# Wide attention in a decoder kernel: a VectorE mask, exponentials with sums on ScalarE, and weights turned in a score bank

## What is computed

```python
    q = split_heads(x @ Wq)
    k = split_heads(x @ Wk)
    v = split_heads(x @ Wv)
    q = apply_rope(q)
    k = apply_rope(k)
    sim = jnp.einsum('bid,bjd->bij', q, k) * scale
    causal = jnp.tril(jnp.ones((t, t), dtype=bool))
    sim = jnp.where(causal[None], sim, -jnp.inf)
    attn = jax.nn.softmax(sim, axis=-1)
    out = jnp.einsum('bij,bjd->bid', attn, v)
    out = out.reshape(b, h, t, d).transpose(0, 2, 1, 3).reshape(b, t, h * d)
    return out @ Wo + bo
```

## Time and profile before

| | us |
|---|---|
| median of 3 runs | 1153.3 (1153.07 to 1155.71) |
| the profiled execution, its own time | 1154.45 |
| its span, first to last instruction | 1152.7 |
| the wide attention in it, about | 594 to 1012 |
| one block of four items in its loop | 24.03 and 24.14, in turn |

### The profile page before, as it was taken

How to read it: one execution, slowest core, us unless ns; L and a number is a source line. 1 busy time by engine, 2 the same in 40 slices (tenths; PEclk the granted TensorE clock), 3 DMA queues, 4 the chain that set the end, 5 groups by cost and what they waited for, 6 DMA issues and landing times. The chain is left out here.

```text
span 1152.7 us, 38659 instructions
## 1 busy us (share of the span) xinstructions
PE 995.0 (86%) x14758; PEld 803.4 (70%) x14759; DVE 844.9 (73%) x2021; ACT 588.4 (51%) x982; POOL 574.4 (50%) x711
## 2 busy tenths in 40 slices
PE   5999999999945799999947989999999999868464
PEld 2666666667632799999945878888888888746213
DVE  4878787888749244444426989999999999568686
ACT  3665656677720466666612444444444444447555
POOL 4232424353300433333225888888888886533424
PEclk9999999999965799999977999999999999955555
DMA  8200000000000111111230000000000000041002
GB/s 256 100 2 0 2 11 20 20 20 28 11 28 0 36 50 47 47 47 47 43 112 10 15 10 12 11 9 11 11 11 11 9 11 1 2 111 56 0 1 74
DMA packets 36985, 37.61 MB, mean 33 GB/s; under 512 B 7142, under 2 KB 31145, under 8 KB 36522
## 3 DMA queue, kind: packets, MB, share of 16 engines
q1 hardware_dynamic: 31690, 27.33, 7.8%
q0 software_dynamic: 4352, 8.92, 3.1%
q10 hardware_dynamic: 866, 0.33, 0.1%
HBM read 27.65 MB, written 8.91 MB: 32 GB/s over the span
## 5 line engine op out<-in xcount | busy, mean ns | idle before, releaser
L1283 POOL DMA_INDIRECT e_x<-xn_rows,e_where x72 | 68.1, 946 | 168.7 <-DVE e_where L1264 120.5
L360 POOL TENSOR_SCALAR n_KX<-n_KT,n_of_head 128x512 f32<-128x512 f32 x124 | 83.8, 698 | 122.0 <-ACT n_KT L601 85.2
L1253 DVE COPY e_y<-e_Y_ps 128x128 f32<-128x128 f32 x72 | 21.0, 291 | 113.8 <-PE e_Y_ps L1220 112.5
L760 DVE TENSOR_REDUCE n_row_max<-n_S_ps 128x16 f32<-128x1024 f32 x64 | 78.1, 1221 | 26.3 <-PE n_S_ps L451 26.3
L1440 POOL TENSOR_TENSOR a_E<-a_E,a_rsum 128x512 f32<-128x512 f32 x64 | 66.6, 1040 | 57.5 <-DVE a_rsum L1804 57.5
L665 ACT ACTIVATE n_ET<-n_ET_ps 128x1024 f32<-128x1024 f32 x64 | 65.5, 1023 | 46.5 <-PE n_ET_ps L461 45.6
L461 PEld LDWEIGHTS n_ET_ps<-ident,n_E 128*128 128x128 f32 x512 | 57.1, 142 | 34.9 <-issue 20.1
L764 DVE TENSOR_TENSOR n_E<-n_S_ps,n_row_max 128x1024 f32<-128x1024 f32 x64 | 78.4, 1225 | 2.9
L1210 PE MATMUL e_G_ps<-e_xT,e_gate_here 128*128 128x128 f32 x576 | 78.4, 280 | 0.9 <-ACT e_up_here L1173 0.9
L1220 PE MATMUL e_Y_ps<-m_down_w,e_hT 128*128 x576 | 77.2, 277 | 1.6 <-issue 1.5
L1210 PE MATMUL e_U_ps<-e_xT,e_up_here 128*128 128x128 f32 x576 | 77.8, 279 | 0.0
(11 more groups left out here) (281 smaller groups left out, 2679.2 us busy)
## 6 DMA issues: line engine op xcount, KB each, us to landing
slot_out<-e_y SPq DMA_DIRECT2D x72, 64.0 KB
X<-in_x SPq DMA_DIRECT2D x8, 256.0 KB, 5.4
n_ctxT<-in_ctxT SPq DMA_DIRECT2D x8, 256.0 KB, 3.3
m_gate_w<-in_L_ffn_gate_w SPq DMA_DIRECT2D x1, 2048.0 KB, 7.4
m_up_w<-in_L_ffn_up_w SPq DMA_DIRECT2D x1, 2048.0 KB, 13.4
...
```

Source lines behind the costliest of these rows:

```text
L360: last = nc.gpsimd.tensor_scalar(KX[:, p, :, h * T:(h + 1) * T], src, of_head[:, h:h + 1], 1.0, ALU.mult, ALU.mult)
L760: nc.vector.tensor_reduce(row_max[:, u % 2, :], src, AX.X, ALU.max).then_inc(max_done, 1)
L1283: nc.gpsimd.indirect_dma_start(out=x[:, j, :], out_offset=None, in_=k.xn_rows, in_offset=bass.IndirectOffsetOnAxis(ap=where[:, j, :], axis ...
```

## The change

For each item:

- The mask is no longer put into PSUM by TensorE. The first score matmul into a bank now starts the accumulation. `subtract_max` becomes `mask_scores`: VectorE multiplies the scores by `SCALE` and adds the table `future` (0 or -1e30) in one SCALAR_TENSOR_TENSOR from PSUM into `E`, and then takes the negated row maximum of `E` into `low`, from SBUF.
- `exponentials` is eight ACTIVATEs of 64 elements in place of one of 512. Each has the column of `low` for its head and half as its bias, and an accumulator output into `row_sum`. The TENSOR_REDUCE of the sums in `reciprocals` is gone, the reciprocal stays.
- The turned weights go into the first score bank, `S_ps[:, 0]`. The K projection has a bank of its own (`K_ps`), and the next block's input is turned in the second score bank. `transpose_e` waits for `masked` of the next item, and `scores` waits for `et_ready` of the item two back.
- The order within a step changes on four engines. TensorE turns the weights after the V projection. ScalarE has two of the exponentials, V, the turned weights, two, then (in g = 0 and 2) the block's own copy, four, and last the weighed values. VectorE starts a step with `reciprocals` of n (before, it did that of n+1 in the middle of the step). GpSimd normalises n (before, n+1) and rotates K of n+2 (before, n+3) ahead of Q of n+3.
- One more table of 64 KB is loaded among the weights.

The diff; a line of dots stands for what is left out:

```diff
+        future = sb("future", [P, P])
...
-        row_max = sb("row_max", [P, 2, GH * UB])
...
+        low = sb("low", [P, 2, GH * UB])
...
-        KE_ps = ps("KE", [P, 512])
+        K_ps = ps("K", [P, 512])
...
         def _(sp):
-            for dst, name in [(wq, "L1_attn_wq"), (wk, "L1_attn_wk"), (cos, "c_cos"), (sin, "c_sin"), (wv, "L1_attn_wv"),
+            for dst, name in [(wq, "L1_attn_wq"), (wk, "L1_attn_wk"), (cos, "c_cos"), (sin, "c_sin"), (future, "c_future"),
+                              (wv, "L1_attn_wv"),
...
-                normalise_e(0, 0)
-                rotate_k(0, 2)
...
-                    if g + 1 < G or nxt:
-                        normalise_e(*item_at(blk, g + 1))
+                    normalise_e(blk, g)
+                    if g + 2 < G or nxt:
+                        rotate_k(*item_at(blk, g + 2))
...
-                        rotate_k(*item_at(blk, g + 3))
...
-                    pe.wait_ge(d_ready, nb * G - 2)
+                    pe.wait_ge(masked, nb * G - 2)
...
-                    mm = nc.tensor.transpose(S_ps[:, 0, u * P:(u + 1) * P], xn[:, u, :], k.ident[:])
+                    mm = nc.tensor.transpose(S_ps[:, 1, u * P:(u + 1) * P], xn[:, u, :], k.ident[:])
...
-                if later(n_, 3):
-                    pe.wait_ge(et_ready, n_ - 2)
...
-                    mm = nc.tensor.matmul(KE_ps[:, a * TOK:(a + 1) * TOK], wk[:, g, a, :], xnT[:], start=True, stop=True)
+                    mm = nc.tensor.matmul(K_ps[:, a * TOK:(a + 1) * TOK], wk[:, g, a, :], xnT[:], start=True, stop=True)
...
-                    pe.wait_ge(d_ready, n_)
+                    pe.wait_ge(masked, n_)
+                if later(n_, 2):
+                    pe.wait_ge(et_ready, n_ - 1)
...
-                for h in range(GH):
-                    half = slice(64 * (h % 2), 64 * (h % 2) + 64)
-                    for b in range(2):
-                        nc.tensor.matmul(S_ps[64 * b:64 * b + 64, h, 0:P], k.causal_queries[half, 0:T], k.causal_keys[half, 0:P],
-                                         start=True, stop=False)
...
-                                                      RK[rows, g % 2, a, tok], start=False, stop=(a == 1 and u == UB - 1))
+                                                      RK[rows, g % 2, a, tok], start=(a == 0 and u == 0),
+                                                      stop=(a == 1 and u == UB - 1), skip_group_check=True)
...
             def transpose_e(blk, g):
...
-                pe.wait_ge(pk_ready, at_most_all(n_ + 3))
+                pe.wait_ge(masked, at_most_all(n_ + 2))
...
-                    mm = nc.tensor.transpose(KE_ps[:, h * P:(h + 1) * P], E[:, g % 2, h * P:(h + 1) * P], k.ident[:])
+                    mm = nc.tensor.transpose(S_ps[:, 0, h * P:(h + 1) * P], E[:, g % 2, h * P:(h + 1) * P], k.ident[:])
...
             def prologue():
...
-                for g in range(3):
-                    project_q(0, g)
-                    if g == 0:
-                        project_v(0, 0)
-                    project_k(0, g)
-                    if g == 1:
-                        scores(0, 0)
+                project_q(0, 0)
+                project_k(0, 0)
+                project_v(0, 0)
+                project_q(0, 1)
+                project_k(0, 1)
+                scores(0, 0)
+                project_q(0, 2)
+                project_k(0, 2)
...
             def step(blk, prev, nxt):
...
-                    transpose_e(blk, g)
...
+                    transpose_e(blk, g)
...
-                                     S_ps[:, 0, 0:TOK].rearrange("c (u b t) -> c u b t", u=UB, b=2), ACT.Copy)\
+                                     S_ps[:, 1, 0:TOK].rearrange("c (u b t) -> c u b t", u=UB, b=2), ACT.Copy)\
...
-            def exponentials(blk, g):
-                act.wait_ge(d_ready, blk * G + g + 1)
-                nc.scalar.activation(E[:, g % 2, :], E[:, g % 2, :], ACT.Exp, scale=SCALE).then_inc(e_ready, 1)
+            def exponentials(blk, g, heads):
+                n_ = blk * G + g
+                act.wait_ge(max_ready, n_ + 1)
+                if later(n_, 2):
+                    act.wait_ge(rsum_ready, n_ - 1)
+                for j in range(heads[0] * UB, (heads[-1] + 1) * UB):
+                    e = E[:, g % 2, j * T:(j + 1) * T]
+                    last = nc.scalar.activation(e, e, ACT.Exp, bias=low[:, g % 2, j:j + 1], accum_out=row_sum[:, g % 2, j:j + 1])
+                if heads[-1] == GH - 1:
+                    last.then_inc(e_ready, 1)
...
             def evacuate_e(blk, g):
...
-                nc.scalar.activation(ET[:, g % 2, :], KE_ps[:], ACT.Copy).then_inc(et_ready, 1)
+                nc.scalar.activation(ET[:, g % 2, :], S_ps[:, 0, :], ACT.Copy).then_inc(et_ready, 1)
...
-                exponentials(0, 0)
+                exponentials(0, 0, range(GH))
...
             def step(blk, p, prev, nxt):
...
+                    if g + 1 < G or nxt:
+                        exponentials(*item_at(blk, g + 1), range(1))
+                        evacuate_v(*item_at(blk, g + 1))
...
-                        exponentials(*item_at(blk, g + 1))
-                    if g + 1 < G or nxt:
-                        evacuate_v(*item_at(blk, g + 1))
+                        exponentials(*item_at(blk, g + 1), range(1, 2))
+                    if nxt and g == 0:
+                        evacuate_xT(blk + 1)
...
-                    if nxt and g == 0:
-                        evacuate_xT(blk + 1)
+                    if g + 1 < G or nxt:
+                        exponentials(*item_at(blk, g + 1), range(2, GH))
...
-                products(KE_ps[:], PK).then_inc(pk_ready, 1)
...
-            def subtract_max(blk, g):
...
+                products(K_ps[:], PK).then_inc(pk_ready, 1)
...
+            def mask_scores(blk, g):
...
-                src = S_ps[:, :, 0:P].rearrange("p h (u t) -> p h u t", t=T)
-                top = row_max[:, g % 2, :].rearrange("p (h u) -> p h u", u=UB)
-                nc.vector.tensor_reduce(top, src, AX.X, ALU.max).then_inc(max_ready, 1)
...
-                dve.wait_ge(max_ready, n_ + 1)
-                nc.vector.tensor_tensor(E[:, g % 2, :].rearrange("p (h u t) -> p h u t", u=UB, t=T), src,
-                                        top.unsqueeze(3).broadcast_to([P, GH, UB, T]), ALU.subtract).then_inc(d_ready, 1)
+                e = E[:, g % 2, :].rearrange("p (j t) -> p j t", t=T)
+                nc.vector.scalar_tensor_tensor(out=E[:, g % 2, :].rearrange("p (h k) -> p h k", h=GH), in0=S_ps[:, :, 0:P],
+                                               scalar=SCALE, in1=future[:].unsqueeze(1).broadcast_to([P, GH, P]),
+                                               op0=ALU.mult, op1=ALU.add).then_inc(masked, 1)
+                if later(n_, 2):
+                    dve.wait_ge(e_ready, n_ - 1)
+                dve.wait_ge(masked, n_ + 1)
+                nc.vector.tensor_reduce(low[:, g % 2, :], e, AX.X, ALU.max, negate=True).then_inc(max_ready, 1)
...
             def reciprocals(blk, g):
...
-                nc.vector.tensor_reduce(row_sum[:, g % 2, :], E[:, g % 2, :].rearrange("p (j t) -> p j t", t=T), AX.X, ALU.add)\
-                    .then_inc(sum_ready, 1)
...
-                dve.wait_ge(sum_ready, n_ + 1)
...
+                mask_scores(0, 0)
...
-                subtract_max(0, 0)
...
-                reciprocals(0, 0)
...
             def step(blk, p, prev, nxt):
...
+                    reciprocals(blk, g)
...
-                        subtract_max(*item_at(blk, g + 1))
+                        mask_scores(*item_at(blk, g + 1))
...
-                    if g + 1 < G or nxt:
-                        reciprocals(*item_at(blk, g + 1))
-                    if g + 3 < G or nxt:
...
+        "c_future": np.tile(np.where(t[None, :] > t[:, None], NEG, 0.0), (2, 2)).astype(np.float32),
```

5 lines of the change are left out of this document (2 added, 3 removed).

## The result

The changed kernel takes 1182.94 us (median of 4 runs, 1181.43 to 1184.38) against 1153.18 before: ratio 1.0257, 95% interval 1.0239 to 1.0275. It is 2.6% slower, 29.8 us. The forecast was 1147.3 with a range up to 1182. The profiled run took 1181.98 us, with a span of 1180.2.

A forecast was written before the change was run, and what follows sets the result against it. VectorE was taken to bound at 6.02 us an item; the new step of 5.88 saves 8.4 us over 60 steps, less 2.4 at the end. From 1154.45 that gives 1148.45, as a median 1147.3 us; range 1129 to 1182.

The forecast's parts named there:

- The bound before: In the wide attention before the change, VectorE sets the pace at 6.02 us an item; TensorE's step is 5.75.
- VectorE's sum: VectorE's work per item in the wide attention, falling from 6.02 to 5.24 us without the sum over `E`.
- The range's end of 0.75: Upper bound in us for VectorE's new mask instruction, from a similar instruction reading a scalar from memory; 0.69 was taken.
- x = 0.34: Cost in us of one new exponential on ScalarE, start to start, with an overlapping second instruction reading its sum.
- Loop A: Two-step loop of waits: Q's projection waits for ScalarE's copy of the weighed values; 4.52 + 4x, 5.88 us a step.
- GpSimd does the same work: Step claiming GpSimd's work stays 20.8 us a block, 5.2 an item, below TensorE's floor.
- The floor of 5.59: TensorE's step in us without mask matmuls, 5.53, with the input's turn once in four; the limit if nothing else binds.
- the gain of 6.0: Whole-kernel saving in us: 8.4 over 60 steps, less 2.4 at the end of the phase.
- rival 2: On ScalarE the sum's reading waits for the exponential's end, 0.43 us each: 22.9 us more, 1176; chance 0.33.
- The argument falls: Signs against the forecast: VectorE stays full, mask takes much over 0.75 us, or GpSimd's order makes scores wait for K.

The follow-up runs named there:

- the written-out loop: The kernel before with TensorE's loop over the blocks written out and nothing else: 1149.88 us, ratio 1.0032.
- the early gather's kernel: The changed kernel with GpSimd's gather moved between the rotations of K and of Q, nothing else: 1149.64 us, ratio 1.0014.

## Why the prediction was wrong, point by point

- **The bound before** (VectorE, TensorE close behind) holds in the main: the written-out loop gave nothing while VectorE was full. But taking the mask matmuls alone away gave 0.55%, so TensorE was closer than "0.27 behind".
- **VectorE's sum** holds: mask 690 ns and maximum 686 as taken. The range's end of 0.75 for the mask wasn't needed.
- **x = 0.34** was right: 0.33. A second instruction per sum exists, and it overlaps as all neighbours do. The Trainium skill's page VectorE: DVE Perf Modes (section "Two Vector instructions with no wait between them") states it for VectorE; the row with 192 ns shows it for ScalarE.
- **Loop A, 5.88 us a step**, holds where nothing covers it: with the gather early and the loop written out a block is 23.72 us, 5.93 a step. Its sign is seen in Q's wait for the copied weighed values.
- **The step that failed**, with most of the 35.6 us between 1147.3 and 1182.94, is one sentence: "GpSimd does the same work [...] and stays under the floor." The work is the same, 20.7 us a block. But the diff moved the gather with the rotations, and I priced the move by the engine's own time only, at nothing. It was worth 28 us of the 29.8. What a moved step takes along, here its DMA, was not worked out, and no rival held it.
- **The floor of 5.59** was read from a step that nothing disturbs, and no row said under which conditions it is. The earlier trace rows were taken with the gather under other instructions. It was also a little low: the undisturbed steps in the last blocks of the changed kernel, without gather or input's turn, take 5.70 where it had 5.53. The forecast did not rest on it, since loop A was longer.
- **A second, small miss**: the block boundary of TensorE's loop, 0.38 us a block, 5 us in all, was covered by VectorE before and is not after. With it the sum of 1147.3 would have been near 1153; the early gather's kernel lies at 1154.8 by its ratio of 1.0014. That kernel is what the prediction had priced, and by it the gain of 6.0 us was not there either.
- **The rivals**: rival 2's time (1176) is close to the result, but x was not its 0.43, and its sign is there only in part. It asked for VectorE idle ahead of the reciprocal for about 1 us a step; that wait is 0.44, and the mask behind it waits 0.77 more for the scores. A time that fits is no mechanism that fits.
- **"The argument falls ... if GpSimd's new order makes the scores wait for K"**: the order was indeed the cause, but by another way. The scores waited for K's rotation 0.7 us in all.
